# Scores of a two-layer block: each head contracted alone in a 64-row half of the array, without the queries' zero blocks

## What is computed

```python
q = (x @ Wq.T + bq).reshape(b, l, h, hd).transpose(0, 2, 1, 3)
k = (x @ Wk.T + bk).reshape(b, l, h, hd).transpose(0, 2, 1, 3)
scores = jnp.einsum('bhqd,bhkd->bhqk', q, k) / math.sqrt(hd)
scores = jnp.where(causal, scores, -jnp.inf)
att = jax.nn.softmax(scores, axis=-1)
out = jnp.einsum('bhqk,bhkd->bhqd', att, v)
```

## Time and profile before

| | us |
|---|---|
| time, median of 3 runs | 716.8 (713.62 to 717.78) |
| span of the profiled execution | 711.7 |
| end of layer one and turn of the last tokens | about 244 to 283 |
| projections, stores and loads of the stacks | about 283 to 350 |
| values and linear layer, with the first maxima | 350 to 417 |
| eight groups of heads | 417 to 686 |
| end of the output projection | 686 to 712 |
| PE busy | 635.7 (89% of the span) |
| DVE busy | 419.8 (59%) |
| ACT busy | 293.8 (41%) |

### The profile page before, as it was taken

How to read it: one execution, slowest core, us unless ns; L and a number is a source line. 1 busy time by engine, 2 the same in 40 slices (tenths; PEclk the granted TensorE clock), 3 DMA queues, 4 the chain that set the end, 5 groups by cost and what they waited for, 6 DMA issues and landing times.

```text
span 711.7 us, 8799 instructions
## 1 busy us (share of the span) xinstructions
PE 635.7 (89%) x3176; PEld 444.5 (62%) x3176; DVE 419.8 (59%) x1139; ACT 293.8 (41%) x498; POOL 86.3 (12%) x107
## 2 busy tenths in 40 slices
PE   3999999999999927983899999999989998999985
PEld 2788888778888715762687865545545555554553
DVE  5676543365532395622497588787878787881003
ACT  4545432243322302121321156656564656477530
POOL 2000000000000086000000350202110201022010
PEclk9999999999999976998799999999998999899998
DMA  6333232011011110469601024515151515111113
GB/s 209 119 113 99 85 118 89 29 60 60 29 60 60 44 45 1 124 204 209 233 29 58 7 46 77 114 42 112 42 113 40 114 42 113 40 32 45 45 29 129
DMA packets 24635, 58.03 MB, mean 82 GB/s; under 512 B 7136, under 2 KB 7648, under 8 KB 24560
## 3 DMA queue, kind: packets, MB, share of 16 engines
q1 hardware_dynamic: 24304, 56.90, 28.9%
q0 software_dynamic: 288, 0.58, 0.4%
HBM read 42.39 MB, written 15.07 MB: 81 GB/s over the span
## 4 chain that ended last, share of the span: by engine, by line
PE 68%; DMA 13%; DVE 9%; ACT 5%; SPq 2%; issue 1%; POOLq 0%; POOL 0%; ACTq 0%; DVEq 0%
PE bank L1088 9%; PE bank L1105 8%; PE slot L1020 8%; PE bank L860 7%; PE slot L860 7%; PE bank L862 7%; PE bank L861 7%; PE slot L861 7%; PE slot L862 7%; DMA u_dram<-u_sb 4%; DMA heads_dram<-attn_lo 4%; DMA den<-u_dram 3%; ACT probs L844 3%; DVE probs L1187 2%; DVE slot L1415 2%
## 5 line engine op out<-in xcount | busy, mean ns | idle before, releaser
L1415 DVE CUSTOM_DVE_ANT_0 slot<-slot,causal 128x512 f32<-128x512 f32 (+3 forms) x384 | 204.4, 584 | 39.6 <-PE slot L1020 37.6
L844 ACT ACTIVATE probs<-bank 128x512 f32<-128x512 f32 (+1 forms) x304 | 155.2, 580 | 96.8 <-PE bank L1088 96.2
L860 PE MATMUL slot<-xt_hi,ring_hi 128*128 128x512 f32 (+2 forms) x248 | 100.0, 403 | 20.5 <-DVE attn_lo L1370 17.0
L1020 PE MATMUL slot<-kst,qst 112*128 112x512 f32 (+3 forms) x288 | 97.1, 364 | 11.5 <-DVE maxcol L1415 8.2
L1088 PE MATMUL bank<-qst,kst 114*128 114x512 f32 (+3 forms) x288 | 98.7, 384 | 4.6 <-ACT probs L844 3.7
L861 PE MATMUL slot<-xt_lo,ring_hi 128*128 128x512 f32 (+2 forms) x248 | 99.0, 399 | 0.0
L862 PE MATMUL slot<-xt_hi,ring_lo 128*128 128x512 f32 (+2 forms) x248 | 98.9, 399 | 0.0
L1088 PEld LDWEIGHTS bank<-qst,kst 114*128 114x128 f32 x288 | 52.0, 192 | 62.3 <-ACT probs L844 51.4
L1105 PE MATMUL bank<-probs,v_sb 128*17 128x512 f32 (+3 forms) x768 | 83.3, 507 | 0.6 <-POOL probs L657 0.6
L1020 PEld LDWEIGHTS slot<-kst,qst 112*128 112x128 f32 x288 | 57.2, 200 | 23.0 <-DVE maxcol L1415 10.7
L860 PEld LDWEIGHTS slot<-xt_hi,ring_hi 128*128 128x128 f32 (+2 forms) x248 | 47.7, 192 | 33.3 <-issue 19.7
(11 more groups left out here) (186 smaller groups left out, 916.8 us busy)
## 6 DMA issues: line engine op xcount, KB each, us to landing
stage<-in_stream SPq DMA_DIRECT2D x43, 512.0 KB, 3.4
heads_dram<-attn_hi SPq DMA_DIRECT2D x8, 512.0 KB
heads_dram<-attn_lo SPq DMA_DIRECT2D x8, 512.0 KB
u_dram<-u_sb SPq DMA_DIRECT2D x16, 256.0 KB, 4.3
qst<-heads_dram SPq DMA_DIRECT2D x12, 256.0 KB, 4.9
kst<-heads_dram SPq DMA_DIRECT2D x12, 256.0 KB, 7.8
stage<-u_dram SPq DMA_DIRECT2D x16, 128.0 KB
stage<-den_dram SPq DMA_DIRECT2D x16, 128.0 KB
```

The costliest lines, as they stand in the source:

```text
L844: act.activation(probs[:, to:to + heads, 0:n], bank[b % 3][:, 0:heads * n].rearrange("p (h n) -> p h n", n=n), ACT.Exp, scale=HD ** -0.5). ...
L860: pe.matmul(out_ap, a[0], b[0], start=start, stop=False)
L1020: pe.matmul(bank_of(("max", u))[:, 0:n], queries(g, hh % 2)[0:DOT_ROWS, hh // 2, i * P:(i + 1) * P], keys(g)[0:DOT_ROWS, hh // 2, c:c + n] ...
L1415: dve.tensor_tensor_reduce(score, score, causal[:, mask:mask + n], 1.0, -3.0e38, ALU.add, ALU.max, to).then_inc(S["max_free"], 1)
```

## The change

Queries become like keys: a stack of 48 rows for each head, at rows 0 or 64, two heads (`hh % 2`) side by side in the free dimension. A head's score is contracted over its own rows alone: 48 for the maxima, 50 for the score, at partition 0 (heads 0 and 1) or 64 (heads 2 and 3). The zeros and their fills go. All three stacks have tiles of their own, and only their keys are filled with ones, on POOL, after the last `normalize`. Of `v_sb` only the column of ones is filled. The head order in scores and in maxima is 0, 2, 1, 3, so that successive matmuls use different halves; two heads of different halves never share a bank, and a step of 128 columns takes two banks and two exponentials where it took one.

```diff
-DOT_ROWS = SIDE + QK_ROWS
-ST_ROWS = DOT_ROWS + 2
+ST_ROWS = QK_ROWS + 2
+STACKS = 3
+
+HEAD_ORDER = (0, 2, 1, 3)
...
-MAX_UNITS = [(i, hh, c, min(512, (i + 1) * P - c)) for i in range(NT) for hh in range(GH)
-             for c in range(0, (i + 1) * P, 512)]
+MAX_UNITS = [(i, hh, c, min(512, (i + 1) * P - c)) for i in range(NT) for c in range(0, (i + 1) * P, 512)
+             for hh in HEAD_ORDER]
...
-    return {P: 4, 2 * P: 2}.get(step_width(s), 1)
+    return 2 if step_width(s) <= 2 * P else 1
+
+
+def score_bank(s, place):
+
+    hh = HEAD_ORDER[place]
+    return (place, 0) if per_bank(s) == 1 else (hh // 2, hh % 2)
...
-        qst = sb(block1, "qst", [P, 2, GH, TOK], F32R)
-        kst = sb(block1, "kst", [P, 2, 2, TOK], F32R)
+        qst = sb(block1, "qst", [P, STACKS, 2, TOK], F32R)
+        kst = sb(block1, "kst", [P, STACKS, 2, TOK], F32R)
...
+        def head_rows(hh, rows):
+            side = hh // 2
+            return slice(SIDE * side, SIDE * side + rows)
...
-            def blank(g):
-
-                for side in range(2):
-                    pool.memset(queries(g, side).rearrange("p b n -> p (b n)").bitcast(F32), 0.0
-                                ).then_inc(S["blank"], 1)
+            pool.memset(v_sb[:, :, :, HD:].rearrange("p t h d -> p (t h d)"), 1.0).then_inc(S["k_ones"], 1)
+            pool.wait_ge(S["xn_ready"], 2 * NT)
+            for g in range(STACKS):
                 pool.memset(keys(g).rearrange("p b n -> p (b n)").bitcast(F32), 1.0).then_inc(S["blank"], 1)
-
-            blank(0)
-            pool.memset(v_sb[:], 1.0).then_inc(S["k_ones"], 1)
-            blank(1)
...
-            for side in range(2):
-                pool.memset(queries(2, side).rearrange("p b n -> p (b n)").bitcast(F32), 0.0).then_inc(S["blank2"], 1)
...
-                pe.matmul(bank_of(("max", u))[:, 0:n], queries(g, hh % 2)[0:DOT_ROWS, hh // 2, i * P:(i + 1) * P],
-                          keys(g)[0:DOT_ROWS, hh // 2, c:c + n], start=True, stop=True).then_inc(S["max_ready"], 1)
+                rows = head_rows(hh, QK_ROWS)
+                pe.matmul(bank_of(("max", u))[:, 0:n], queries(g)[rows, hh % 2, i * P:(i + 1) * P],
+                          keys(g)[rows, hh % 2, c:c + n], start=True, stop=True).then_inc(S["max_ready"], 1)
...
-            dve.wait_ge(S["y_done"], NT)
-            dve.memset(keys(2).rearrange("p b n -> p (b n)").bitcast(F32), 1.0).then_inc(S["blank2"], 1)
```

More of the change, by code:

```diff
@@ L376, in build, with queries @@
             "den_landed0 den_landed1 den_inverted den_stored "
-            "attn_f attn_hi_ready attn_lo_ready y_biased y_added o_ready out_sb_ready stored dve k_ones blank blank2 "
+            "attn_f attn_hi_ready attn_lo_ready y_biased y_added o_ready out_sb_ready stored dve k_ones blank "
         ).split()}
[L380 to L384, removed]
+        def queries(g):
+            return qst[:, g % STACKS]
         def keys(g):
-            if g % 3 == 2:
-                return xt_hi[:, KD - 2:, :]
-            return kst[:, g % 3]
+            return kst[:, g % STACKS]
+        def head_rows(hh, rows):
+            side = hh // 2
+            return slice(SIDE * side, SIDE * side + rows)
         def slot_of(user):
@@ L501, in stack @@
                     sp.wait_ge(S["st_ready"], banks_before(g - 2, 0))
[L502 to L505, removed]
+                if g < STACKS:
+                    sp.wait_ge(S["blank"], g + 1)
                 for n, which in enumerate("qk"):
@@ L508, in stack @@
                     for side in range(2):
-                        first = heads_dram[m, n, GH * (g % 2) + side]
-                        st = queries(g, side) if which == "q" else keys(g)
+                        first = heads_dram[m, n, GH * (g % 2) + 2 * side]
+                        st = queries(g) if which == "q" else keys(g)
                         for row, rows in ((0, 2 * HD), (2 * HD, HD)) if which == "q" else ((0, HD), (HD, 2 * HD)):
@@ L514, in stack @@
                                          bass.AP(first.tensor, first.offset,
-                                                 [[TOK, rows], [2 * 2 * HD * TOK, 2], [1, TOK]])
+                                                 [[TOK, rows], [2 * HD * TOK, 2], [1, TOK]])
                                          ).then_inc(S[f"stacks{z}"], 16)
@@ L534, in neg_max @@
                     first = max_dram[g, 0, 2 * side]
-                    sp.dma_start(queries(g, side)[DOT_ROWS:ST_ROWS].bitcast(F32),
+                    at = SIDE * side + QK_ROWS
+                    sp.dma_start(queries(g)[at:at + 2].bitcast(F32),
                                  bass.AP(first.tensor, first.offset, [[GH * TOK, 2], [1, 2 * TOK]])
@@ L839, in _ @@
                         act.wait_ge(S["y_added"], NT)
-                    for hh in range(0, GH, heads):
-                        b = banks_before(g, s) + hh // heads
+                    for place in range(GH // heads):
+                        b = banks_before(g, s) + place
+                        hh = HEAD_ORDER[place] if heads == 1 else heads * place
                         to = (GH * (STEPS * g + s) + hh) % NPROB
@@ L1072, in _, with score @@
                 linear(t)
-            def score(g, s, hh):
+            def score(g, s, place):
                 half, j = QSTEPS[s]
-                heads = per_bank(s)
-                b = banks_before(g, s) + hh // heads
+                hh = HEAD_ORDER[place]
+                of, at = score_bank(s, place)
+                b = banks_before(g, s) + of
                 n = step_width(s)
                 q0 = HALF * (half + 1) - n
-                if hh % heads == 0 and b >= 3:
+                if at == 0 and b >= 3:
                     pe.wait_ge(S["exp_done"], b - 2)
@@ L1084, in score @@
                     pe.wait_ge(S["y_free"], NT)
-                if s == 0 and hh == 0:
+                if s == 0 and place == 0:
                     pe.wait_ge(S[f"negm_landed{g % 2}"], 32 * (g // 2 + 1))
-                at = hh % heads * n
-                last = pe.matmul(bank[b % 3][:, at:at + n], keys(g)[0:ST_ROWS, hh // 2, j * P:(j + 1) * P],
-                                 queries(g, hh % 2)[0:ST_ROWS, hh // 2, q0:q0 + n], start=True, stop=True)
-                if hh % heads == heads - 1:
+                rows = head_rows(hh, ST_ROWS)
+                last = pe.matmul(bank[b % 3][:, at * n:(at + 1) * n], keys(g)[rows, hh % 2, j * P:(j + 1) * P],
+                                 queries(g)[rows, hh % 2, q0:q0 + n], start=True, stop=True)
+                if at == per_bank(s) - 1:
                     last.then_inc(S["st_ready"], 1)
```

4 lines of the change are left out of this document (1 added, 3 removed).

## The result

The changed kernel took 747.6 us (median of 4 runs, 745.8 to 753.6); the kernel before, timed beside it, 717.3 (713.6 to 717.9). The ratio is 1.045 (95% interval 1.040 to 1.051): slower by 30 us, where 3.6 were forecast and the range ended at 732. The profiled execution has a span of 744.1 against 711.7, and a mean TensorE clock of 0.883 against 0.952.

The account below looks back on a forecast made before the run. PE was taken to bound `values` and `linear`, PE and DVE together the groups of heads. Terms -15 - 0.8 + 21 - 5.5 + 3.9 = +3.6 on 716.8 gave about 720 us, range 704 to 732.

Parts of the forecast that it names:

- Fills, -15: End of layer one: with POOL's long fills after the normalizes, PE's 12.76 us wait goes; -15 us, bounds -12 and -17.
- Fill on DVE and the switches, -0.8 + 21: DVE's fill at the head of group 0 goes, -0.8; 48-row maxima between full products in `values` and `linear` cost +21.
- The 16-row turns: Eight 16-row transposes in the earlier trace, used to price a switch from full products and back: 0.29 us a return trip.
- Groups at full clock, -7.8 - 1.0 + 1.3: Groups of heads: -7.8 us for groups 1 to 6, -1.0 for group 0, +1.3 for switches at `turn_maxima`.
- I count one more such group, +2: Groups of heads: PE arrives earlier and waits longer, so one more group has PE's clock at half after a wait, +2 us.
- my rivals: No switch cost, 691 us (0.13); groups gain DVE's whole wait, 711 (0.20); no side-by-side halves, 732 (0.13); fills pay half, 727 (0.10).
- Output projection, +3.9: Group 7: 20 new switches between output projection parts and 50-row scores, +3.8 us, and ten more exponentials, +0.1.
- halves do not stream side by side: Groups and `values`: PE's order keeps its length and pairs save nothing, +2.7 + 8.8, 732 us, slower; chance 0.13.
- Slower was the likeliest sign: Whole kernel: slower (above 720.4 us) had chance 0.43, faster (below 713.2) 0.29, same 0.28.

Follow-up runs that it names:

- the kernels that differ in this alone: The changed kernel's order with full rows (705.3 us, ratio 0.988), and the same with 80 early maxima contracted in halves (723.1 us, ratio 1.014).
- The kernel with 66 rows: Changed kernel, heads 2 and 3 taking scores of heads 0 and 1, half the stacks loaded, 66 rows a maximum and 68 a score: 817.8 us, ratio 1.137.
- the kernel in one half: Changed kernel with every maximum and score contracted in rows 0 to 48 (50), heads 2 and 3 taking scores of heads 0 and 1: 853.1 us, ratio 1.196.
- the kernel with 66 and 114 rows: Changed kernel, heads 2 and 3 taking scores of heads 0 and 1, half the stacks loaded, 66 rows a maximum, 114 a score: 685.8 us, ratio 0.959.
- the kernel with half rows from group 5: The changed kernel's order with full rows, but half rows for scores of groups 5 to 7 and maxima of groups 6 and 7: 730.1 us, ratio 1.022.
- the kernel with the fills alone: The kernel before with layer one's query and key fills moved behind the 16th normalize and the first fill cut to the ones column: 703.5 us, ratio 0.986.

## Why the prediction was wrong

**Fills, -15: right.** The router's product moved by 14.55 us and the first maximum by 14.9. One reading behind the term was not exact: the slow normalizes end at 252.68 + 15.73 = 268.41, 1.7 us after the last fill and 0.3 after POOL's first addition, so they stood beside that addition too.

**Fill on DVE and the switches, -0.8 + 21: right.** From first maximum to first score 65.8 us became 86.0, +20.2 as predicted (+21 - 0.8), and the kernels that differ in this alone say +19.9. The 16-row turns were a good stand-in: 1.08 us foreseen for the three distances, 1.09 measured. The Trainium skill, "TensorEngine Tiling (Array Packing)", section Key Properties, has the rule that a change of tiling mode drains TensorE, and the trace agrees. The kernel with 66 rows, which don't fit in a half, has no such loss (66.1 us for this stage). Together with the fills the first score was to come 5.2 us later; it came 5.3 later.

**Groups at full clock, -7.8 - 1.0 + 1.3: the sign was right, but the gain is seen in one group only.** Group 6, at full clock in both, gained 0.7 where 1.3 was forecast. A wide step with maxima (step 4 of a group) went from 2.85 to 2.67 us at full clock, -0.18 where -0.3 was forecast, and one without maxima took 2.66 and takes 2.65. That agrees with steps bound by the exponential and the banks, not by PE's length.

**The step that failed is "I count one more such group, +2".** That term was for PE's half clock. I had read it as a matter of waits alone, from the groups with 0.95 and 0.91 in the earlier trace rows, and asked only whether there would be one more wait. The runs show that in this kernel the clock also hangs on the rows of the matmuls. With 48 and 50 rows, a spell of 3.4 to 6.8 us becomes one of 10 to 38, one comes in group 0 where there was none, and those of groups 3 and 5 begin without a wait for denominators. Groups 0 to 5 grew by 25.3 us, and groups 0 to 6 by 24.6 where -5.5 was the forecast. That miss of 30 us is more than the whole error of the spans, 32.4 - 3.6 = 28.8. None of my rivals had it: the trace of before has no stretch in which most matmuls use few rows, and its bounds were drawn from durations, while the clock that they were read at was taken as given.

**Output projection, +3.9:** the span behind group 6 grew by 2.5. Part of it is again clock: in step 2 of group 7, from 685.7 to 692.5, full products and scores run at half clock, where the kernel before had 1.00.

```profile
690.44 0.58 PE L1087 MATMUL bank<-qst,kst 50*128 50x256 f32 x1
690.95 0.79 PE L857 MATMUL slot<-xt_hi,attn_hi 128*128 128x512 f32 x1
691.54 0.63 PE L858 MATMUL slot<-xt_lo,attn_hi 128*128 128x512 f32 x1
```

Here 691.54 - 690.95 = 0.59 us from a product's first part to its second, where `values` has 346.88 - 346.54 = 0.34.

The rival "halves do not stream side by side" (732) fails too: pairs start together in `values`. Slower was the likeliest sign, but on account of the switches, and the fills paid for most of them.

**What stays open.** Why the changed kernel gets its full clock back in the groups, while the kernel in one half doesn't before group 7, was not tried: overlap of halves, or the waits and columns between, may do it. Nor is it shown which of scores and maxima weighs more; the kernel with 66 and 114 rows says that full scores nearly keep the clock, but in group 4 of the kernel with half rows from group 5 the scores had full rows too, with 48-row maxima between them, and the half clock stayed. That the queries' fills are gone was not tried by itself either.

## What to carry to other kernels

When an edit makes matmuls smaller in rows, columns or count, ask of the clock first: a saving of 0.2 us a step is nothing beside a step that takes 4.1 instead of 2.7. Rows of zeros that seem a waste can be what holds the clock. And a wait of 2 to 4 us on an engine ahead of TensorE may cost twice, once itself and once in the clock behind it: moving the denominators' reciprocal two steps gave 26 us (703.5 to 677.2), more than anything that the change meant to save.

## What the runs showed of the hardware that was not expected

- TensorE busy 368.60 of 368.60 us with 48- and 50-row matmuls between the values' 128-row ones stayed at 1.2 GHz throughout; with 66 and 68 rows 100.00 of 100.00 us likewise; with 112 and 114 rows the same program had 2.4 GHz but for one spell of 6.8 us in the groups, the extra rows holding zeros in the queries.
- A wide step of scores, maxima and values takes 2.85 us with 112 and 114 rows at full clock, 2.67 in halves at full clock, 4.1 in halves at half clock, and 5.1 to 5.4 in one half at half clock (step 4 of the groups, from one step's first values to the next's).
- A 48-row maximum between full products costs 0.39 us a round trip in `values`: 0.10 ahead of it, 0.19 behind it, and 0.10 between the next product's first two parts.
- Eight 120-element products on VectorE took 7.05 us beside GpSimd's additions of biases (the kernel with the fills alone) and 1.64 us behind them (the changed kernel). Ahead of a projection TensorE waited 6.50 us in the first and 0.58 in the second.
